# A graph attention block with a spline layer on one core: the first 128 rows summed in pieces, zero products in TensorE's waits, some constants moved to VectorE

## What is computed

```python
HW = h @ W                                   # h is x, [1250, 512]
s = HW @ a[:512, 0]; t = HW @ a[512:, 0]
e = leaky_relu(s[row] + t[col], 0.2)
m = segment_max(e, row); ex = exp(e - m[row])
den = segment_sum(ex, row)
agg = segment_sum((ex / den[row])[:, None] * h[col], row)
basis = b_splines(agg, grid)                 # 8 cubic pieces per element
out = silu(agg) @ base_w.T + einsum('nip,oip->no', basis, spline_w)
x = layernorm(x + out)
```

## Time and profile before

| | |
|---|---|
| median of 3 runs (402.78 to 403.83) | 403.43 us |
| the profiled execution | 404.09 us |
| its span, first to last instruction | 402.3 us |
| TensorE busy | 377.7 us, 94% |
| VectorE busy | 351.1 us, 87% |
| ScalarE busy | 264.5 us, 66% |
| GpSimd busy | 34.3 us, 9% |
| mean granted clock of TensorE | 0.981 |

### The profile page before, as it was taken

How to read it: one execution, slowest core, us unless ns; L and a number is a source line. 1 busy time by engine, 2 the same in 40 slices (tenths; PEclk the granted TensorE clock), 3 DMA queues, 4 the chain that set the end, 5 groups by cost and what they waited for, 6 DMA issues and landing times.

```text
span 402.3 us, 5037 instructions
## 1 busy us (share of the span) xinstructions
PE 377.7 (94%) x1856; PEld 296.0 (74%) x1856; DVE 351.1 (87%) x436; ACT 264.5 (66%) x273; POOL 34.3 (9%) x109
## 2 busy tenths in 40 slices
PE   4999719999999999999999999999999999999993
PEld 2446507888888888787888888887777777777782
DVE  8999989888876788999899999889999899989254
ACT  2759955566555889976686866777657786755213
POOL 5100110000000000101010101001010101010000
PEclk9999957999999999999999999999999999999999
DMA  7950096000000029455646555623322553723102
GB/s 258 317 166 2 1 172 195 0 2 0 2 0 0 2 74 369 118 145 161 193 117 164 151 159 155 200 63 102 108 81 77 143 159 117 233 76 103 53 28 98
DMA packets 23466, 45.90 MB, mean 114 GB/s; under 512 B 1846, under 2 KB 2058, under 8 KB 23442
## 3 DMA queue, kind: packets, MB, share of 16 engines
q0 software_dynamic: 11872, 23.01, 21.6%
q1 hardware_dynamic: 11570, 22.57, 16.8%
HBM read 43.02 MB, written 2.56 MB: 113 GB/s over the span
## 4 chain that ended last, share of the span: by engine, by line
PE 83%; DVE 13%; issue 2%; DVEq 0%; POOL 0%; ACT 0%; POOLq 0%
PE PS L1189 62%; PE PS L1145 18%; DVE oh L421 5%; DVE still L435 3%; PE PS L1127 3%; PE PS L1155 1%; DVE xl L444 1%; DVE ex L678 0%; DVE scrap L650 0%; DVE bend L459 0%; DVE ex L681 0%; ACT xr L957 0%; DVEq L606 0%; DVE st L772 0%; DVE xr L767 0%
## 5 line engine op out<-in xcount | busy, mean ns | idle before, releaser
L1189 PE MATMUL PS<-wh,s 128*128 128x512 f32 (+1 forms) x720 | 224.6, 392 | 0.1
L1189 PEld LDWEIGHTS PS<-wh,s 128*128 128x128 f32 (+1 forms) x720 | 133.4, 185 | 33.1 <-issue 1.5
L1189 PE MATMUL PS<-wl,s 128*128 128x512 f32 (+1 forms) x360 | 141.1, 392 | 0.0
L1189 PEld LDWEIGHTS PS<-wl,s 128*128 128x128 f32 (+1 forms) x360 | 66.8, 185 | 15.3
L944 ACT ACTIVATE s<-v 128x1280 fp32r<-128x1280 f32 (+1 forms) x32 | 40.0, 1250 | 44.5 <-DVE v L750 25.9
L927 ACT ACTIVATE v<-xt,bias 128x1280 f32<-128x1280 f32 (+1 forms) x32 | 42.9, 1339 | 18.4 <-DVE s L760 17.2
L744 DVE SCALAR_TENSOR_TENSOR v<-v,v 128x1280 f32<-128x1280 f32 (+1 forms) x32 | 46.5, 1454 | 5.1 <-ACT v L930 5.1
L750 DVE SCALAR_TENSOR_TENSOR v<-v,v 128x1280 f32<-128x1280 f32 (+1 forms) x32 | 46.8, 1461 | 3.3
L760 DVE SCALAR_TENSOR_TENSOR s<-v,s 128x1280 fp32r<-128x1280 f32 (+1 forms) x32 | 46.5, 1454 | 3.6 <-ACT s L944 3.6
L412 POOL DMA_DIRECT2D wh<-in_splT x32 | 22.9, 717 | 276.7 <-PE PS L1189 180.0
L746 DVE SCALAR_TENSOR_TENSOR v<-v,v 128x1280 f32<-128x1280 f32 (+1 forms) x32 | 46.5, 1453 | 0.0
(11 more groups left out here) (138 smaller groups left out, 351.4 us busy)
## 6 DMA issues: line engine op xcount, KB each, us to landing
wh<-in_splT POOLq DMA_DIRECT2D x32, 512.0 KB, 4.1
wring<-in_splT SPq DMA_DIRECT2D x21, 512.0 KB, 3.9
xt<-in_xT SPq DMA_DIRECT2D x1, 2500.0 KB, 11.8
xh<-in_x POOLq DMA_DIRECT2D x1, 2304.0 KB, 10.0
out<-xr SPq DMA_DIRECT2D x9, 256.0 KB
wh<-in_baseT POOLq DMA_DIRECT2D x4, 512.0 KB, 5.4
xl<-in_x POOLq DMA_DIRECT2D x1, 1536.0 KB, 13.5
wring<-in_baseT SPq DMA_DIRECT2D x3, 512.0 KB, 4.4
```

Source lines behind the costliest of these rows:

```text
L1189: m = e.matmul(PS[0:rows(w), w % 8, :], sx[:, ic, tl * 128:tl * 128 + rows(w)], wx[:, ic, :], start=first and n == 0, stop=last and n == 2)
```

## The change

Five things.

- *Constants.* The 22 memsets of `reach_col` and the one of C's padding leave GpSimd's row and become VectorE's first instructions, with a semaphore of their own, `s_reach`.
- *Biases in four steps.* ScalarE stores 0.8 s in place of s (`s_part`), and `small` needs four steps instead of five; r1 is the third, as the fourth was before.
- *Order in block 0.* VectorE takes `weigh(0, 0)` ahead of `small(1)`, and `weigh(1)` and the p_low steps in another order. ScalarE takes `p_high(0, 0)` ahead of `e1(1)`, and `e2(1)` ahead of `p_high(0, 1)`; `e2(3)` goes behind `p_high(2)`. On TensorE `aggregate` becomes `sums(j, i, p)`, one kind of product of one piece; block 0 takes the high parts of each piece, both with xh and xl, as they come, and the low parts last, behind `turn(1)`.
- *Zero products.* `keep_warm(n)` issues n products of `nought`, 128 x 500, into a PSUM bank that nothing reads; 32 of them stand between the last counts and the first sums.
- *In the counts.* Negations two batches earlier, the spreading of t three batches later, and the two register loads on VectorE one by one behind batches 18 and 19 instead of together behind batch 20.

```diff
-        TB_AT = (14, 14, 15)
+        TB_AT = (17, 17, 18)
-        NEGATIVE_AT = {13 + k: k for k in range(ADDED)}
+        NEGATIVE_AT = {11 + k: k for k in range(ADDED)}
...
@@ gpsimd
-            e.memset(C[:, :, N:RP], 0).then_inc(s_setup, 1)
-            for b in range(NCP // TB):
-                m = e.memset(reach_col[:, TB * b:TB * b + TB], float(REACH[b] ** 2) if b < NB else 0.0)
-            m.then_inc(s_setup, 1)
@@ vector
+            for b in range(NCP // TB):
+                m = e.memset(reach_col[:, TB * b:TB * b + TB], float(REACH[b] ** 2) if b < NB else 0.0)
+            m.then_inc(s_reach, 1)
+            e.memset(C[:, :, N:RP], 0).then_inc(s_reach, 1)
...
-                if b == SIZES_AT:
+                if b == SIZES_AT - 2:
                     e.wait_ge(s_tab, TABLE)
-                    first, behind = loaded(e, r_size, 0, 2, 0, NC + 1)
+                    first = loaded(e, r_size, 0, 1, 0, NC)[0]
+                if b == SIZES_AT - 1:
+                    behind = loaded(e, r_size, 1, 2, 1, NC + 1)[0]
...
                 e.wait_ge(s_small, n + 1)
-                e.tensor_tensor(y, s, t, ALU.add).then_inc(s_small, 1)
+                e.scalar_tensor_tensor(out=y, in0=t, scalar=-SLOPE, in1=s8, op0=ALU.mult, op1=ALU.add
+                                       ).then_inc(s_small, 1)
                 e.wait_ge(s_small, n + 2)
-                e.scalar_tensor_tensor(out=m, in0=y, scalar=SLOPE, in1=y, op0=ALU.mult, op1=ALU.max
+                e.scalar_tensor_tensor(out=r1, in0=t, scalar=-1.0, in1=y, op0=ALU.mult, op1=ALU.min
                                        ).then_inc(s_small, 1)
                 e.wait_ge(s_small, n + 3)
-                e.tensor_tensor(r1, s, m, ALU.subtract).then_inc(s_small, 1)
-                e.scalar_tensor_tensor(out=r2, in0=s, scalar=SLOPE, in1=m, op0=ALU.mult, op1=ALU.subtract
-                                       ).then_inc(s_small, 1)
+                e.tensor_tensor(r2, r1, s8, ALU.subtract).then_inc(s_small, 1)
...
             greatest(1)
+            weigh(0, 0)
             small(1)
-            weigh(0, 0)
             weigh(0, 1)
-            inverse(0)
             p_low(0, 0)
             greatest(2)
+            weigh(1)
+            p_low(0, 1)
             small(2)
-            p_low(0, 1)
-            weigh(1)
+            p_low(1)
+            inverse(0)
             inverse(1)
             weigh(2)
             inverse(2)
-            p_low(1)
             greatest(3)
@@ scalar
-                        e.copy(scol[:, lo // 128:hi // 128],
-                               PS[:, 6 + k % 2, lo // 64:hi // 64].rearrange("p (j a) -> p j a", a=2)[:, :, 0]
+                        e.mul(s_part[:, lo // 128:hi // 128],
+                              PS[:, 6 + k % 2, lo // 64:hi // 64].rearrange("p (j a) -> p j a", a=2)[:, :, 0], 1 - SLOPE
...
+            p_high(0, 0)
             e1(1)
-            p_high(0, 0)
+            e2(1)
             p_high(0, 1)
-            e2(1)
+            p_high(1)
             e1(2)
             e2(2)
-            p_high(1)
             normalise(0)
             e1(3)
-            e2(3)
             for j in range(1, NT - 1):
...
                 p_high(j + 1)
+                if j == 1:
+                    e2(3)
@@ tensor
+            def keep_warm(n):
+                for k in range(n):
+                    e.matmul(PS[:, 6, 0:CW], nought[:, 0:128], nought[:, :], start=True, stop=True)
+
             e.wait_ge(s_scol, 3)
+            e.wait_ge(s_trow, 3)
+            keep_warm(8)
...
+            keep_warm(6)
+            e.wait_ge(s_tmax, 1)
+            keep_warm(8)
+            e.wait_ge(s_e1, 1)
+            keep_warm(4)
+            e.wait_ge(s_e2, 1)
+            keep_warm(4)
             turn(0, 0)
+            keep_warm(2)
+            sums(0, 0, 0)
             turn(0, 1)
-            for j in range(NT):
-                aggregate(j, 0, 2)
+            sums(0, 2, 0)
+            sums(0, 0, 1)
+            sums(0, 2, 1)
+            turn(1)
+            sums(0, 1, 0)
+            sums(0, 1, 1)
+            for j in range(1, NT):
+                sums(j, 0)
+                sums(j, 1)
                 if j + 1 < NT:
                     turn(j + 1)
-                aggregate(j, 2, 3)
-                if j:
-                    back(j - 1)
+                sums(j, 2)
+                back(j - 1)
```

52 lines of the change are left out of this document (26 added, 26 removed).

## The result

The changed kernel took **402.5 us** (median of 20 executions, 401.4 to 403.22) beside 403.48 for the kernel before on the same chip (20 executions, 402.4 to 404.42): ratio 0.9977, 95% interval 0.9968 to 0.9987. Measured twice more, each time beside the kernel before on one chip, the ratio was 0.9968 (0.9955 to 0.9981) and 0.998 (0.9971 to 0.9989). It is faster, by 1.0, 1.6 and 0.7 us; 2.27 were forecast. (One execution of the kernel before, on the chip of the run two_only, took 1337.17 us and stands in no ratio.) The first profiled execution of the changed kernel took 401.40, the fastest of its 20. So I read it beside four more traces of the same kernel, of 402.22, 402.84, 402.24 and 402.10 us.

What follows compares the result with a forecast made beforehand. The chain was TensorE for 83% of the span and VectorE for 13%, VectorE's part being the first 61 us. Gains of 1.57 (blocks, after the new wait) and 0.70 (front) make 2.27: 403.43 to 401.2 us, range 400.0 to 403.2.

Steps and rivals of the forecast that it cites:

- the eight zero products ahead of the left-over tile: TensorE after the counts: they end within about a tenth of the tile being ready; zero to 0.3 us lost, none summed.
- Constants: Start of VectorE: 23 memsets leave GpSimd, cost VectorE 1.54 us plus 0.2 for C; 0.7 us gained.
- Rival 3: VectorE's memsets at the start are held as bend was; front loses 1.6 us, 403.5 us in all; chance 0.08.
- Table loads: VectorE's two register loads in the counts, moved to batches 18 and 19, cost zero; at most 0.8 us.
- Clock: TensorE between counts and first transposes: zero products keep 2.4 GHz, granted clock 1.00 from 48 to 70 us.
- rival 2: Zero products do not hold TensorE's clock, which falls ahead of tmax; slower, 405.1 us; chance 0.08.
- Blocks: First attention blocks: block 0 and turn(1) done 2.7 us sooner; 1.57 us left after a wait in block 2.
- The new wait: TensorE waits 1.05 us for ph(2), until 79.05, as ScalarE's copy stands behind e1(3), which waits for small(3).
- Rival 1: No TensorE wait for ph(2): the whole 2.6 us stays, 3.3 with the front, 400.1 us; chance 0.12.
- After the blocks: Spline products and tail: no loss put in the sum; ph(3) is ready before it is wanted, so nothing follows.
- The profiled execution of the kernel before: Page read at 404.09 us, the runs' median 0.66 lower at 403.43; the difference was carried over to the median.

Runs made afterwards that it cites:

- two_only: Changed kernel with ScalarE's copy of block 2's factors ahead of block 3's first exponential and five zero products instead of eight ahead of the left-over tile: 400.9 us, ratio 0.9931.
- front_zero: Kernel before with the memsets on VectorE and all 32 zero products, but its old order of blocks and counts: 403.15 us, ratio 0.9978.
- five_again: Changed kernel with five zero products instead of eight ahead of the left-over tile, measured again on another chip: 401.49 us, ratio 0.994.
- fewer_zero: Changed kernel with five zero products instead of eight ahead of the left-over tile, first measurement: 401.67 us, ratio 0.9942.
- no_zero: Changed kernel without any of its 32 zero products: 403.66 us, ratio 0.9987.
- copy_first: Changed kernel with ScalarE copying block 2's factors before it takes block 3's first exponential: 401.83 us, ratio 0.9948.
- constants_back: Changed kernel with the 23 memsets back on GpSimd, all else as changed: 404.33 us, ratio 1.0013.
- front_only: Kernel before with the 23 memsets on VectorE and nothing else: 403.02 us, ratio 0.9974.
- before_again: The kernel before, unchanged, measured once more: 404.39 us, ratio 1.0002.
- ring_late: Changed kernel with block 2's copy first, five zero products ahead of the left-over tile, residual's rows later and third unit's low weights held back: 400.72 us, ratio 0.9917.
- best: Changed kernel with block 2's copy first, five zero products instead of eight ahead of the left-over tile, and the residual's rows loaded later: 400.73 us, ratio 0.9916.

## Why the prediction was wrong

The median was 1.3 us above the forecast's 401.2, inside the range, and the gain 0.98 us instead of 2.27. The step that failed is a term that was put at nothing: the eight zero products ahead of the left-over tile, "zero to 0.3 lost" and zero in the sum. Step by step:

- **Constants: right in direction, mis-sized.** 0.7 was taken; it is 1.05. The memsets cost VectorE 0.66 us, not 1.54, and nothing on the path: bend and its fellows start where they did, not 0.7 later. Rival 3 (held memsets) is excluded by their 0.03 us each.
- **Table loads: what the failed step left out.** "The two register loads ... cost zero" was said of VectorE's, and is right of them. TensorE's own register load, between the last count and the zero products, was left out of the working. In the new order it takes 1.24 to 1.69 us instead of 0.49.
- **Zero products ahead of the left-over tile: the step that failed.** They were to end when the tile was ready. Behind the short load they do (front_zero, 0.45 as before); behind the long one they end too late, and the hold is 0.29 to 0.59 us more than before in five traces. With five of them the gain is there: 403.83 to 401.49 is 2.34 us. That this comes so near to 2.27 is in part luck, for its terms are others: in five_again's trace 1.05 for the front, 0.10 lost to the hold, 1.54 for the blocks and 0.04 later, 2.53 together. The traces show 0.3 to 0.6 of what the three products cost; the medians show 0.9 on one chip, and 0.0028 to 0.0040 of ratio, 1.1 to 1.6 us, between chips. The rest is open. The second unit's weights are the other place at which the traces differ, but they do not follow the zero products: the gap there was 0, 0, 0.43, 0.53 and 0.85 in the five traces of the changed kernel, 0 in five_again, 0.26 in fewer_zero and two_only, 0.65 in front_zero, and 0.80 in no_zero, which has no zero product at all.
- **Clock: right.** 1.00 from 48 to 70 us in all traces of the changed kernel, with zeros as operands and a longest gap of 1.70 us between them (forecast 1.4). This is as the Trainium skill has it (TensorE: Matmul & The Clock Gate, What's actually happening), which names activity and not values. What was not foreseen is that the mean clock is lower in a few executions (0.985 to 0.993 in 6 of 121 executions of kernels with zero products); in the one of them that was traced, fewer_zero, it fell in the counts, long before the place at which rival 2 had it.
- **Blocks: right in the traces.** Relative to the first greatest, block 0's closing transposes came 2.7 us sooner (forecast 2.7) and block 1's 1.53 (1.57). The new wait was 0.91 us and ended at 78.10; the forecast had 1.05 ending at 79.07, or 78.4 once its 0.7 for the front is taken off. It stands at the named link and has the named reason; copy_first shows it. Rival 1 (no new wait) fell. In the medians this gain cannot be seen with eight zero products (constants_back).
- **After the blocks: not in the sum.** The second unit's weights were late by 1.20 us already in both traces of the kernel before, about the 1.14 that VectorE has to spare, and in the changed kernel by 1.22 to 2.00: 0 to 0.85 lost. They are issued when block 9's sums are done, so they move with the work; why they came in time in both traces of the kernel before and late in most others is not shown.
- **The profiled execution of the kernel before.** Its 404.09 stood 0.6 above its runs' median and its clock was at 1.2 GHz for 13.65 us, where front_only and no_zero had 10.24 (from the granted clock by stretch); before_again had the longer stretch too. The forecast carried its working over to the median unchanged. front_only, with the shorter half-speed stretch, ended 1.80 us sooner than before_again, of which the front is 1.05; in the median it gave 1.0 against the kernel before on that chip, and 1.4 against before_again's own. How much of this is in the medians is not settled, and I make no term of it.

## What to carry to other kernels

A filler that keeps an engine's clock stands in that engine's queue: count everything ahead of it, the queue's own register loads too, and give it less than the wait it fills, since its surplus delays the work behind it in full (here by the register load's length less 0.51). When a profile says that one engine's wait is going away, ask for each later transfer how much slack it has: one that is late by as much as its slack, as the weights here with 1.20 against 1.14, has none left to give. And a kernel whose executions vary by over a microsecond is read from several traces, not from the one at hand, which here was the fastest of twenty.

## What the runs showed that was not expected

- 22 memsets of a few elements on VectorE take 0.66 us together (0.03 each), while two tiny tensor_scalar operations start 0.07 apart, and none of the 22 was held, though GpSimd was at work beside them (two iotas, 0.85 to 1.63 us).
- The same register load of TensorE takes 0.49 us in one order of the counts and 1.24 to 1.69 in another.
- TensorE's clock fell to half in the middle of the counts in one traced execution of a kernel whose other executions keep it. The six executions with a lower mean clock took 1.7 to 3.6 us more than the median of their kernel.
- A transfer of 512 KB of weights lands in 4.7 us with one transfer of low weights beside it (ring_late), in 7.4 with the next two transfers of low weights too (best), and in 8.6 with the residual's rows as well (two_only).
